# One block of WKV attention and eight-expert layer on one core: where gathered rows are transposed and split, ahead of a tile's products or inside them

## What is computed

```python
def _L0_attn_ref(x, ...):
    xk = x_prev + (x - x_prev) * tmk          # xv, xr in the same way
    k = einsum(xk, Wk) + bk; v = ...; r = ...
    wkv = _wkv_scan(k, v, time_decay, time_first)
    return einsum(sigmoid(r) * wkv, Wo) + bo

def _L0_ffn_ref(x, wg, W, b):                  # W: 8 experts, 512 x 512
    probs = softmax(x @ wg)
    idx = argmax(probs); gate = probs[idx]
    return gate * (einsum(x, W)[idx] + b[idx])   # one expert per token

x = layernorm(x + _L0_attn_ref(x, ...))
x = layernorm(x + _L0_ffn_ref(x, ...))
```

## Time and profile before

| | us |
|---|---|
| median of three runs | 614.51 |
| lowest, highest | 614.08, 618.14 |
| the profiled execution, its own time | 619.29 |
| its span in the profile | 616.8 |
| TensorE matmul busy | 572.7 (93%) |
| VectorE busy | 532.3 (86%) |
| ScalarE busy | 421.9 (68%) |
| GpSimd busy | 279.8 (45%) |

### The profile page before, as it was taken

The page is one execution under the profiler, slowest core; times in us unless marked ns, Lnnn a source line. Parts: engine busy times, 40 slices in busy tenths (PEclk is TensorE's granted clock), DMA queues, the critical chain, the costliest instruction groups (busy, mean ns, idle before and its releaser), DMA issues. The chain is left out here.

```text
span 616.8 us, 8911 instructions
## 1 busy us (share of the span) xinstructions
PE 572.7 (93%) x2404; PEld 409.5 (66%) x2405; DVE 532.3 (86%) x854; ACT 421.9 (68%) x799; POOL 279.8 (45%) x221
## 2 busy tenths in 40 slices
PE   4998789999999999999999999999979999989891
PEld 1444566677677768668767866874658778767680
DVE  5889989998998999999899899889997888665670
ACT  3637656677587677668658766776966676776782
POOL 2767515544453552454545255311051566555531
PEclk9998799999999999999999999999979999999996
DMA  9352540093056019107504710955664686866640
GB/s 342 136 69 71 209 64 0 1 251 92 0 183 143 19 39 249 52 0 215 111 14 170 138 34 14 275 204 158 251 190 113 205 253 202 254 192 212 187 164 1
DMA packets 40979, 84.40 MB, mean 137 GB/s; under 512 B 8751, under 2 KB 8751, under 8 KB 40818
## 3 DMA queue, kind: packets, MB, share of 16 engines
q1 hardware_dynamic: 30482, 56.67, 27.8%
q0 software_dynamic: 10464, 27.33, 19.7%
HBM read 66.95 MB, written 35.65 MB: 166 GB/s over the span
## 5 line engine op out<-in xcount | busy, mean ns | idle before, releaser
L1166 POOL TENSOR_TENSOR mixed<-unsplit,mixed 128x1024 fp32r<-128x1024 f32 x42 | 100.0, 2404 | 118.3 <-ACT mixed L775 118.3
L705 PE MATMUL y_ps<-w_e_hi,xgT 128*128 x312 | 109.4, 412 | 4.2 <-DVE yo L1828 3.4
L539 PE MATMUL y_ps<-w_o,rw 128*128 128x512 f32 x224 | 100.8, 594 | 0.0
L526 PE MATMUL vb<-mixed,w_kvr 128*128 128x512 f32 x336 | 88.3, 413 | 6.0 <-DVE evn L1373 5.9
L526 PE MATMUL kb<-mixed,w_kvr 128*128 128x512 f32 x336 | 83.8, 399 | 5.8 <-POOL mixed L1166 3.1
L526 PE MATMUL rb<-mixed,w_kvr 128*128 128x512 f32 x336 | 87.0, 408 | 0.9 <-DVE ee L1387 0.9
L526 PEld LDWEIGHTS vb<-mixed,w_kvr 128*128 128x128 f32 x336 | 63.5, 193 | 23.9 <-DVE evn L1373 8.0
L526 PEld LDWEIGHTS kb<-mixed,w_kvr 128*128 128x128 f32 x336 | 63.1, 191 | 21.9 <-DVE state L1341 5.1
L526 PEld LDWEIGHTS rb<-mixed,w_kvr 128*128 128x128 f32 x336 | 62.8, 189 | 19.7 <-issue 5.7
L1182 POOL TENSOR_TENSOR ee<-ee,state 128x512 f32<-128x512 f32 x32 | 34.9, 1092 | 87.7 <-DVE state L1357 87.1
L1324 DVE SCALAR_TENSOR_TENSOR unsplit<-diff,vec,xb 128x512 f32<-128x512 f32 x96 | 68.0, 772 | 5.2 <-PE kb L526 5.0
(11 more groups left out here) (234 smaller groups left out, 1089.4 us busy)
## 6 DMA issues: line engine op xcount, KB each, us to landing
bias<-b_experts SPq DMA_DIRECT2D x39, 256.0 KB
x_biased<-bo POOLq DMA_DIRECT2D x8, 1024.0 KB, 17.6
w_e_raw<-w_experts SPq DMA_DIRECT2D x8, 1024.0 KB, 8.0
rows<-x_biased SPq DMA_DIRECT2D x28, 256.0 KB, 3.5
x_rows<-rows SPq DMA_DIRECT2D x28, 256.0 KB, 6.5
xb<-xT SPq DMA_DIRECT2D x4, 1026.0 KB, 5.3
xb<-xT SPq DMA_DIRECT2D x3, 1024.0 KB, 5.1
w_raw<-w_square SPq DMA_DIRECT2D x2, 1024.0 KB, 10.4
```

Source lines behind the costliest of these rows:

```text
L526: mm = pe.matmul(bank, w_kvr[m][:, a, h, o:o + P], mixed[m][:, bb, h, :], start=(k == 0), stop=(k == 3 * CH - 1))
L539: mm = pe.matmul(y_ps[:, j % 2, :], rw[:, half, c, j * P:(j + 1) * P], w_o[:, c, :], start=(c == 0), stop=(c == CH - 1))
L705: mm = pe.matmul(y_ps[:, n % 2, :], xgT[n % 3][:, a, c, :], w[:, bass.ds(p, 1), c, :].rearrange("p u o -> p (u o)"), start=(c == 0 and (a, ...
L1166: pool.tensor_tensor(mixed[m][:, LO, 2 * hp:2 * hp + 2, :], unsplit[m][:, LO, 2 * hp:2 * hp + 2, :], mixed[m][:, HI, 2 * hp:2 * hp + 2, :] ...
```

## The change

It moves work and adds none. `STEADY` is 7.

1. TensorE, head: the output projection of the last block's tile 3 goes behind the logits and transposes that followed it and behind the transposes of expert tile 0.
2. TensorE, steps: for k+2 of 7 and more `turn(k+2)` is issued inside `expert(k)`, behind nine of its twelve products.
3. The last block's transposes of its tiles 2 and 3 go from behind expert tile 1 to behind tile 2, their logits from behind tile 2 to behind tile 3.
4. ScalarE, head: the copies of the block before and of expert tile 0 go ahead of the last block's normalization; that of the last block's tiles 2 and 3 goes behind further copies and writes its squares to another buffer, `squares`, for which it waits for the logits of the last block but one.
5. ScalarE, steps: for k+3 of 7 and more the copy of tile k+3 comes behind the normalization of tile k.
6. VectorE, head: the low halves of experts 4 and 5 go behind the splits of tiles 0 and 1, and the split of tile 2 ahead of experts 6 and 7.
7. VectorE, steps: for k+3 of 7 and more the split of tile k+3 comes behind the addition of tile k+1, ahead of the routing arithmetic that follows it.

```diff
@@ -695,7 +696,7 @@
             def place_of(numbers, k):
                 return pe.value_load(numbers[0:1, bass.ds(k, 1)], min_val=0, max_val=EXPERTS - 1)
 
-            def expert(k, n, p, following=()):
+            def expert(k, n, p, following=(), turned_next=None):
 
                 ahead = []
                 pe.wait_ge(turned_lo, k + 1)
@@ -707,6 +708,8 @@
                                        start=(c == 0 and (a, w) == (HI, w_e_hi)), stop=(c == CH - 1 and a == LO))
                     if c == 1:
                         ahead = [place_of(numbers, m) for numbers, m in following]
+                    if c == 2 and turned_next is not None:
+                        turn(*turned_next)
                 mm.then_inc(expert_filled, 1)
                 return ahead
 
@@ -720,30 +723,34 @@
             out_last(2)
             logits(before, 1, late_ps[:, 1, :])
             turn_rows(before, 2)
-            out_last(3)
             logits(before, 2, late_ps[:, 2, :])
             turn_rows(before, 3)
             pe.wait_ge(d_ready, CHUNKS)
             turn(0, 0, 0)
+            out_last(3)
             logits(before, 3, late_ps[:, 3, :])
             turn(1, 0, 1)
             pe.wait_ge(tiles_ready, 1)
 
             ahead = [place_of(expert_full, 0), place_of(slot_full, 0)]
             for k in range(FULL):
-                turn(k + 2, (k + 2) // RING, (k + 2) % RING)
+                later = (k + 2, (k + 2) // RING, (k + 2) % RING)
+                if k + 2 < STEADY:
+                    turn(*later)
 
                 pe.wait_ge(we_split, ahead[0] + 1)
-                ahead = expert(k, k % RING, ahead[1], ((expert_full, k + 1), (slot_full, k + 1)) if k + 1 < FULL else ())
+                ahead = expert(k, k % RING, ahead[1], ((expert_full, k + 1), (slot_full, k + 1)) if k + 1 < FULL else (),
+                               later if k + 2 >= STEADY else None)
                 if k == 0:
                     turn_last(0)
                     turn_last(1)
                 if k == 1:
                     logits_last(0)
                     logits_last(1)
+                if k == 2:
                     turn_last(2)
                     turn_last(3)
-                if k == 2:
+                if k == 3:
                     logits_last(2)
                     logits_last(3)
                 if k == 4:
@@ -757,14 +764,13 @@
                 ahead = [place_of(slot_mixed, r * RING)]
                 for m in range(RING):
                     k = FULL + m
-                    turn(r * RING + (k + 2), r + (k + 2) // RING, (k + 2) % RING)
-                    ahead = expert(r * RING + k, k % RING, ahead[0], ((slot_mixed, r * RING + (m + 1)),) if m + 1 < RING else ())
+                    ahead = expert(r * RING + k, k % RING, ahead[0], ((slot_mixed, r * RING + (m + 1)),) if m + 1 < RING else (),
+                                   (r * RING + (k + 2), r + (k + 2) // RING, (k + 2) % RING))
...
@@ -1018,10 +1024,10 @@
                 act.wait_ge(shifted, turn)
                 act.activation((gate_e, gate_e2)[turn - 1][:], (lg, lg2)[turn - 1][:], ACT.Exp).then_inc(gate_exp, 1)
 
-            def squares_of(source, q):
+            def squares_of(source, q, scratch=ev2):
 
                 wait(act, row_squared, q)
-                act.activation(ev2[:], source, ACT.Square, bias=mean[:, q:q + 1],
+                act.activation(scratch[:], source, ACT.Square, bias=mean[:, q:q + 1],
                                accum_out=rstd[:, q % TPB:q % TPB + 1]).then_inc(row_squared, 1)
 
             def deviation_before(h):
@@ -1040,7 +1046,11 @@
 
             def deviation_last(j):
                 act.wait_ge(row_means, j + 1)
-                squares_of(rows_last[:, j], TPB + j)
+                if j < 2:
+                    squares_of(rows_last[:, j], TPB + j)
+                else:
+                    act.wait_ge(logits_done, last * TPB)
+                    squares_of(rows_last[:, j], TPB + j, squares)
                 act.wait_ge(row_squared, TPB + j + 1)
                 act.activation(rstd[:, j:j + 1], rstd[:, j:j + 1], ACT.Ln, bias=eps_t[:], scale=1.0 / H).then_inc(var_ln, 1)
                 act.wait_ge(var_ln, last * 2 + (j + 1))
@@ -1056,6 +1066,11 @@
             def move_last(j):
                 act.wait_ge(row_turned, last * TPB + (j + 1))
                 act.activation(x1T_last[:, j % 2], last_banks[j % 2].rearrange("p (c q) -> p c q", c=CH), ACT.Copy).then_inc(x1T_moved, 1)
+
+            def move_gathered(k, n):
+                act.wait_ge(turned, k + 1)
+                wait(act, expert_filled, k - 2)
+                act.activation(xgT[n % 3][:, HI], turned_ps[n % 2], ACT.Copy).then_inc(turned_hi, 1)
 
             reciprocal_guess(before, 1)
             deviation(earlier, 1)
@@ -1105,17 +1120,11 @@
             expert_hi(5)
             act.wait_ge(y_filled, last * TPB)
             expert_hi(6)
+            move_turned(before, 2)
+            move_turned(before, 3)
+            move_gathered(0, 0)
             deviation_last(0)
             norm_last(0)
-            move_turned(before, 2)
-            deviation_last(1)
-            norm_last(1)
-            move_turned(before, 3)
-
-            def move_gathered(k, n):
-                act.wait_ge(turned, k + 1)
-                wait(act, expert_filled, k - 2)
-                act.activation(xgT[n % 3][:, HI], turned_ps[n % 2], ACT.Copy).then_inc(turned_hi, 1)
 
             def norm2(k, n):
                 act.wait_ge(mean2_ready, k + 1)
@@ -1128,35 +1137,39 @@
                 act.activation(yo[n][:], yo[n][:], ACT.Identity, bias=nmr2[:, n:n + 1],
                                scale=rstd2[:, n:n + 1]).then_inc(out_ready, 1)
 
-            move_gathered(0, 0)
+            deviation_last(1)
+            norm_last(1)
             move_gathered(1, 1)
             act.wait_ge(y_filled, TILES)
             expert_hi(7)
+            move_gathered(2, 2)
+            move_last(0)
+            move_last(1)
             deviation_last(2)
             norm_last(2)
             deviation_last(3)
             norm_last(3)
-            move_gathered(2, 2)
-            move_last(0)
-            move_last(1)
             for k in range(FULL):
-                move_gathered(k + 3, (k + 3) % RING)
-                if k == 0:
+                if k + 3 < STEADY:
+                    move_gathered(k + 3, (k + 3) % RING)
+                if k == 1:
                     move_last(2)
                     move_last(3)
                 norm2(k, k % RING)
+                if k + 3 >= STEADY:
+                    move_gathered(k + 3, (k + 3) % RING)
                 if k == 3:
                     gates_of(2)
             rounds = (MIXED - 3) // RING
             with act.Fori(0, rounds) as r:
                 for m in range(RING):
                     k = FULL + m
+                    norm2(r * RING + k, k % RING)
                     move_gathered(r * RING + (k + 3), (k + 3) % RING)
-                    norm2(r * RING + k, k % RING)
...
@@ -1746,8 +1759,6 @@
             add_last(1)
             expert_lo(2)
             expert_lo(3)
-            expert_lo(4)
-            expert_lo(5)
 
             def choose_late():
                 largest(EARLY, LATE, late_ps, lg2)
@@ -1837,20 +1848,26 @@
             def step(r, n):
 
                 k = r * RING + n
-                split_gathered(k + 3, (n + 3) % RING)
+                early = isinstance(k, int) and k + 3 < STEADY
+                if early:
+                    split_gathered(k + 3, (n + 3) % RING)
                 add_bias(k + 2, r + (n + 2) // RING, (n + 2) % RING)
                 shift2(k, n)
                 add_gathered(k + 1, (n + 1) % RING)
+                if not early:
+                    split_gathered(k + 3, (n + 3) % RING)
 
             split_gathered(0, 0)
             add_last(2)
+            expert_lo(4)
+            split_gathered(1, 1)
+            expert_lo(5)
             add_last(3)
-            split_gathered(1, 1)
+            split_gathered(2, 2)
             expert_lo(6)
             expert_lo(7)
             add_bias(0, 0, 0)
             add_bias(1, 0, 1)
-            split_gathered(2, 2)
             add_gathered(0, 0)
             dve.wait_ge(row_turned, last * TPB)
             for j in range(TPB):
@@ -1886,18 +1903,18 @@
             with dve.Fori(0, rounds) as r:
                 for m in range(RING):
                     k = FULL + m
-                    split_gathered(r * RING + (k + 3), (k + 3) % RING)
                     add_bias(r * RING + (k + 2), r + (k + 2) // RING, (k + 2) % RING)
                     shift2(r * RING + k, k % RING)
                     add_gathered(r * RING + (k + 1), (k + 1) % RING)
+                    split_gathered(r * RING + (k + 3), (k + 3) % RING)
...
```

12 lines of the change are left out of this document (6 added, 6 removed).

## The result

The changed kernel took 620.42 us in the median of eight runs (616.81 to 621.56), the kernel before 614.82 (613.68 to 618.14) on the same chip: a ratio of 1.0068, 95% interval 1.0042 to 1.0094. It became slower, where the prediction had 613.5 and a range of 606.5 to 619.0. On a second and a third chip the ratio was 0.9987 (0.9962 to 1.0012) and 1.0032 (1.0018 to 1.0045).

A forecast was written before the change was run, and what follows sets the result against it. TensorE was the busiest engine (93%), with 6.5 us of waits behind tile 17. Head gain 2.4 less 1.5 for the steps, net 0 later, gave -0.9: 613.6 on the median, put down as 613.5 us, range 606.5 to 619.0.

The forecast's parts named there:

- (a): Front: products of tile 2 start 3.8 us earlier, at 468.5, with VectorE's addition of tile 0 left at 467.6.
- (b): Moved logits and transposes of the last block: tile 4 starts 2.4 us earlier, at 478.1 instead of 480.52.
- rival 4: Ahead of the projection TensorE stands for gathered rows, hidden behind tile 2's wait: nothing on the total; inside the forecast's 0.55.
- Rival 3: TensorE's new stops at the head lower its clock for three tiles: +2.7 us, 616 us; chance 0.12.
- the sum: All terms together: 0.9 us off the profiled 619.3 gives 618.4; on the median 613.6, put down as 613.5 us.
- (c): From tile 4's step, splits stand 0.5 us for ScalarE's copy in nine steps: 1.5 us lost, bounds 0 and 4.5.
- late signals: TensorE's signals seen about 4 us after the work; with following waits, most of the 6.5 us behind tile 17.
- (d): Transposes inside products, tiles 7 to 38: stops for gathered rows go, shadows lose as much; net 0, bounds -6.5 and +2.3.
- Rival 1: Late signals come from stops for gathered rows behind a tile's products and go: 6.5 us less, 607.0; chance 0.25.
- Rival 2: Lateness hits the transposes' signal, as the split comes closer ahead of its products: +4.3 us, 618 us; chance 0.2.
- The 6.5 us of waits behind tile 17: TensorE's waits over 19 tiles, 68.12 us against 61.6: the only large thing to win behind 520 us.

The follow-up runs named there:

- h2: The kernel before, unchanged, measured again beside the changed kernel on a chip without late signals: ratio 1.0009.
- h1: The changed kernel, unchanged, measured a third time, on a chip without late signals: ratio 1.0032 to the kernel before.
- i1: The changed kernel with the low half of expert 5 moved ahead of VectorE's row split of tile 1: ratio 1.0013 to the kernel before.
- h3: The kernel before with only the head of the change (items 1, 3, 4 and 6), steps in the old order: ratio 1.0011.
- f1: The changed kernel, unchanged, measured again on another chip: ratio 0.9987 to the kernel before.
- h4: The changed kernel with TensorE's transposes back between the tiles (item 2 undone): ratio 1.0056 to the kernel before.
- i2: The changed kernel with expert 5's low half ahead of tile 1's row split and the routing of steps 4 to 12 ahead of the split: ratio 1.0011.
- after: The changed kernel itself, here its first trace: ratio 1.0068 to the kernel before.
- e3: The changed kernel with the routing arithmetic of steps 4 to 12 ahead of the split again: ratio 1.0044 to the kernel before.
- e2: The kernel before with only the steps of the change (items 2, 5 and 7), head in the old order: ratio 1.0024.
- batches g to i: Third to fifth batches of follow-up runs, variants of both kernels on two chips without late signals: ratios 0.9994 to 1.0077 to the kernel before.

## Why the prediction was wrong

**(a) and (b), the head: 2.4 us expected, 0.2 measured (63.0 to 62.8 us from scan to addition 4, h2 and h1).** The step that failed reads: the change "adds and removes nothing, so I leave that addition at 467.6". It adds no work, but it takes the cover of two weight splits from ahead of VectorE's first two row splits, which then stand for ScalarE's copies whenever TensorE's clock was low before 448 us (0.40 and 1.68 us in h1). The gain from tile 0 to tile 4 came, 2.5 us, and paid for it. Tile 2 stood for the addition, and there was no stop for gathered rows, so rival 4 did not arise.

Rival 3, the clock, was put at a chance of 0.12 and is the term that was missing. No trace of this head has the full clock from 440 to 476 us. It was low either ahead of the two splits or behind tile 2, where it costs 2.4 us (16.2 against 13.8 us from addition 0 to 4 in i1 and h1), near the 2.7 put down. That is so in h3 and i1 and, in part, in the changed kernel itself (f1: 0.64 from 468 to 472, 16.2 us). An estimate for a trace with neither is 46.7 + 13.8 = 60.5 us to tile 4, 2.5 less than h2, which is what was forecast; the nearest are h4 and i2 with 61.6. By this estimate the orders do what the sum said, and the clock takes it back. That tile 0 and tile 4 still fell within 1 us of their forecast times in the first trace is partly luck: its first layer ended 1.45 us earlier than in the trace before (scan at 419.46 and 420.91), which hides most of the 2.2. (The queue ahead of tile 0 was summed with the 0.6 of its transposes twice; without it 457.9 comes out, and "about 458" stands.)

**(c), the ring: standing as forecast, its price wrong.** Each split stands 0.50 us behind the copy as the rows said. I let the present idle time of 2.9 us take up most of the 4.5 and put down 1.5. It cost 2.2 us to tile 13 and 0.6 more to tile 17, 2.8 in all, on the chip without late signals. Opening the ring alone gives back 1.4 (after to e3) and 1.1 us (i1 to i2) of the stretch to tile 13, and about 1 stays with item 2, which (d) had put at nothing. Idle time in a ring of waits is no reserve for more of the same: the routing was moved from beside the ring into it.

**(d), the stage behind tile 17: right.** Net 0 was forecast; it is -0.2 us on the chip without late signals, +0.6 in the first pair of traces. Item 2's cost lies ahead of it, between tiles 4 and 13. Stops ahead of transposes are gone as expected. Rival 1 falls: in the first trace, e2 and e3 late signals stand without any stop for gathered rows. Rival 2's mechanism is not seen in the first trace (behind tile 17 no split stands over 0.6 us, no copy over 1.1); what is seen is a chain that I had not thought of: the addition at 551.13 is late, the split of tile 24 stands behind it (552.02), and the products stand for the split. Before, products came 0.9 us after a late addition; now it is 1.8.

**The sum.** -0.9 was forecast; the parts as measured on the chip without late signals are -0.2 + 2.8 - 0.2 = +2.4 us. On the first chip the pair of traces gives +3.8 from scan to addition 37 (183.1 against 179.4): -0.4, +2.5, +1.0, +0.6. The ratio 1.0068 stands for 4.2 us and the two medians lie 5.6 apart; what the first chip adds beyond the +2.4 is not shown. The 6.5 us of waits behind tile 17, which I called the only large thing to win, are not a fixed cost of the kernel: on both chips of batches g to i they don't exist in any trace.

## What to carry to other kernels

Where work is moved between engines' queues, write down the ring of waits that a step closes (here `shift2`, normalization, copy, split), and see for each moved piece whether it lay beside the ring or now lies in it; in the ring it costs its full length. A new order adds waits even where it adds no work, and a delay that the old order covered may show only in executions in which the clock was low. Two executions are compared stretch by stretch in their granted clock before a stop is put down to the order. Take differences inside a trace from a common event, and repeat the kernel before on the chips in question, before waits of a single trace are counted as something to win.
